# A graph layer whose main path is written out behind no branch, with a ring of 12 slots and x and the results in one buffer

## What is computed

```python
agg = segment_sum(edge_attr, dst, 6250)
h   = relu(concat([x, agg, u[0]], axis=1) @ W1 + b1)      # 128+128+16 -> 256
out = h @ W2 + b2 + x
x   = layernorm(x + out)                                   # over the 128 features, no scale
```

## Time and profile before

| | |
|---|---|
| three runs | 190.38, 191.70, 191.78 us; median 191.7 |
| the profiled execution | span 188.2 us from first to last instruction, 6264 instructions; its time beyond the span is not recorded |
| busy | TensorE 163.8 us (87%), VectorE 117.6 (62%), ScalarE 56.8 (30%), GpSimd 31.7 (17%) |
| DMA | 61.90 MB, mean 329 GB/s; main queue at work for 93.5% of the span |
| chain of waits | TensorE 82%, VectorE 8%, issue 3%, DMA 3%, ScalarE 2% |
| VectorE waits for TensorE's turns | 45.3 us in 44 waits |
| SyncE waits for TensorE's sums | 76.9 us in 43 waits |

### The profile page before, as it was taken

One profiled execution on the slowest core, in us unless ns is written; L12 is line 12 of the kernel. 1 busy time (PEld: TensorE's weight loads), 2 busy tenths in 40 slices (PEclk: granted clock), 3 DMA queues, 4 the chain that ended last, 5 costly groups with the idle time before them and its releaser, 6 DMA issues.

```text
span 188.2 us, 6264 instructions
## 1 busy us (share of the span) xinstructions
PE 163.8 (87%) x2207; PEld 115.0 (61%) x2207; DVE 117.6 (62%) x420; ACT 56.8 (30%) x151; POOL 31.7 (17%) x35
## 2 busy tenths in 40 slices
PE   0057952899999999999999999999999999999890
PEld 0046731548658668568568577487586685777690
DVE  5739693224864775765657666656747757477764
ACT  2022412031441442334144235225314423223331
POOL 7800530000200200201002002002002002006712
PEclk9999998599999999999999999999999999999999
DMA  5999954999999999999999999999999999999402
GB/s 110 307 334 374 376 212 140 384 375 337 337 313 376 373 374 374 370 377 374 374 374 373 374 373 374 374 373 373 374 374 372 374 374 374 356 325 387 164 31 67
DMA packets 42185, 61.90 MB, mean 329 GB/s; under 512 B 1975, under 2 KB 39541, under 8 KB 42170
## 3 DMA queue, kind: packets, MB, share of 16 engines
q1 hardware_dynamic: 41046, 61.23, 93.5%
q10 hardware_dynamic: 1124, 0.48, 1.2%
HBM read 58.50 MB, written 3.20 MB: 328 GB/s over the span
## 4 chain that ended last, share of the span: by engine, by line
PE 82%; DVE 8%; issue 3%; DMA 3%; ACT 2%; DVEq 1%; ACTq 0%
PE sum_ps L966 29%; PE turn_ps L979 15%; PE hid_ps L1024 10%; PE out_ps L1070 9%; PE hid_ps L1031 9%; DMA base_row<-in_dst_dram 3%; PE xt_ps L987 2%; PE hid_ps L1043 2%; PE hid_ps L1007 2%; DVE bases L660 2%; DVE onehot L683 1%; PE xt_ps L1070 1%; DVE place L703 1%; DVE local_rows L668 1%; ACT local_t L475 1%
## 5 line engine op out<-in xcount | busy, mean ns | idle before, releaser
L966 PE MATMUL sum_ps<-edge_ring,onehot 128*32 128x128 f32 x1662 | 62.5, 283 | 6.2 <-issue 4.4
L966 PEld LDWEIGHTS sum_ps<-edge_ring,onehot 128*32 128x32 f32 x1662 | 43.0, 112 | 28.7 <-issue 15.5
L712 DVE TENSOR_TENSOR agg_t<-agg_t,turn_ps 128x128 f32 x70 | 19.9, 284 | 45.3 <-PE turn_ps L979 45.3
L683 DVE TENSOR_TENSOR onehot<-iota,local_t 128x384 f32<-128x384 f32 x70 | 38.3, 551 | 11.7 <-issue 9.2
L496 ACT COPY sums<-sum_ps 128x128 f32<-128x128 f32 x70 | 18.8, 268 | 82.4 <-PE sum_ps L966 80.8
L979 PE MATMUL turn_ps<-place,sums 128*128 128x128 f32 (+1 forms) x140 | 34.6, 329 | 0.0
L433 POOL TENSOR_TENSOR xb<-x_sb,half_b 128x512 f32<-128x512 f32 x10 | 12.8, 1277 | 120.0 <-DVE y L737 120.0
L979 PEld LDWEIGHTS turn_ps<-place,sums 128*128 128x128 f32 (+1 forms) x140 | 21.3, 191 | 13.8 <-issue 13.7
L703 DVE TENSOR_SCALAR place<-iota,rel_cols 128x128 f32<-128x128 f32 x70 | 21.1, 301 | 1.7 <-issue 1.7
L1070 PE MATMUL out_ps<-w_sb,hid_t 128*128 128x128 f32 x160 | 21.0, 275 | 0.0
L1024 PE MATMUL hid_ps<-x_t,w_x 128*128 128x512 f32 x40 | 20.4, 630 | 0.0
(11 more groups left out here) (92 smaller groups left out, 111.6 us busy)
## 6 DMA issues: line engine op xcount, KB each, us to landing
edge_ring<-in_edge_attr_dram SPq DMA_DIRECT2D x69, 768.0 KB, 7.2
x_sb<-in_x_dram SPq DMA_DIRECT2D x10, 256.0 KB, 4.9
out_dram<-z SPq DMA_DIRECT2D x1, 2304.0 KB
dst_rows<-in_dst_dram SPq DMA_DIRECT2D x1, 384.0 KB
x_late<-in_x_dram SPq DMA_DIRECT2D x1, 384.0 KB
out_dram<-z_late SPq DMA_DIRECT2D x3, 128.0 KB
out_dram<-z SPq DMA_DIRECT2D x1, 256.0 KB
w_x<-in_L_gnn_W_dram ACTq DMA_DIRECT2D x1, 128.0 KB, 5.0
```

Of the source, the lines that this page charges most:

```text
L683: nc.vector.tensor_tensor(onehot[:, slot], cols, loc, ALU.is_equal).then_inc(onehot_ready, 1)
L712: nc.vector.tensor_tensor(to, to, turn_ps[i % 2][:, 0:SPAN], ALU.add).then_inc(group_added, 1)
L966: last = nc.tensor.matmul(sum_ps[i % 2][c * WIN:(c + 1) * WIN, 0:d], onehot[0:p, i % ONEHOTS, c * R + r], edge_ring[0:p, i, c * R + r], st ...
```

## The change

- The main path has no branch ahead of it and no loop: all 70 groups are written out, step by step. The flag's branch, with a general path that recomputes everything, stands behind the last work of each engine. The check's steps stand at steps 4 to 6 and 9 instead of 0 to 4.
- The ring has 12 slots. SyncE loads group 0 ahead of the second piece of the destinations.
- `x_all` holds x of all nodes, loaded without a wait. GpSimd adds half of b2 in it, y and the normalised rows are written over it, and the result is stored from it.
- Groups are taken in batches of `PAIR` = 1. One-hots and places have 3 buffers; at step b VectorE makes the one-hot of b+2 and the place of b+1, then adds group b-1.
- A block's x and aggregate parts stand together in the step in which it is complete, the output in the next step, the moments behind the step after, the normalisation one step later. ScalarE's root stands ahead of that step's copy.
- The blocks are complete at groups 6, 12, 18, 24, 30, 36, 40, 46, 52 and 59.
- The late pieces' x is loaded at group 53 and turned at steps 58 to 60; its part is multiplied beside the aggregate part. All normalisations are VectorE's.

```diff
+SLOTS = 12
+PAIR = 1
+BUFFERS = 3
-ONEHOTS = 6
-PLACES = 3
-EARLY = 2
-LEAD = 4
...
+    complete_at = [6, 12, 18, 24, 30, 36, 40, 46, 52, 59, 60, 63, 66, 67, 69, n_grp]
...
+    single0 = 60
+    batch_first = list(range(0, single0, PAIR)) + list(range(single0, n_grp)) + [n_grp]
...
+    hidden_step = [batch_first.index(complete_at[n]) for n in range(n_big)]
+    out_step = [b + 1 for b in hidden_step]
+    turn_x_step = [1] + out_step[:n_big - 1]
...
 # SyncE
+            load_group(0)
+
...
+            for g in range(1, n_grp):
+                load_group(g)
+                if g in x_load_at:
+                    load_x(x_load_at[g])
+                if g == x_late_at:
+                    load_x_late()
...
 # ScalarE
+            for b in range(late_step):
+                for n in range(n_big):
+                    if out_step[n] + 2 == b:
+                        root(n)
+                copy_batch(b)
...
+                for n in range(n_big):
+                    if turn_x_step[n] == b:
+                        copy_x_t(n)
+                    if hidden_step[n] == b:
+                        relu(n)
...
 # VectorE
+            def make_onehot(b):
+                g, k = batch_first[b], len(groups(b))
+                if b >= BUFFERS:
+
+                    dve.wait_ge(group_summed, batch_first[b - BUFFERS + 1])
...
+            def step(b):
+                if b == WORST_STEP + 1:
+                    check(3)
+                if b + 2 < n_batch:
+                    make_onehot(b + 2)
+                if b + 1 < n_batch:
+                    make_place(b + 1)
+                if b > 0:
+                    add_batch(b - 1)
+
+            late_step = batch_first.index(single0)
+            for b in range(late_step):
+                step(b)
+                if CHECK0 <= b < CHECK0 + 3:
+                    check(b - CHECK0)
+                for n in range(n_big):
+                    if out_step[n] + 1 == b:
+                        moments(n)
+                    if out_step[n] + 2 == b:
+                        normalize(n)
...
 # TensorE
+            for b in range(late_step):
+                sum_batch(b)
+                if b > 0:
+                    turn_batch(b - 1)
...
+                if b == WORST_STEP:
+                    pe.wait_ge(worst_ready, 1)
+                    pe.wait_ge(y_ready, 1)
+                    nc.tensor.transpose(out_ps[0:1, worst_at], worst[0:n_grp, 0:1],
+                                        ident[0:n_grp, 0:n_grp]).then_inc(worst_turned, 1)
+                for n in range(n_big):
+                    if out_step[n] == b:
+                        sum_out(n)
+                    if turn_x_step[n] == b:
+                        turn_x(n)
+                    if hidden_step[n] == b:
+                        sum_hidden_x(n)
+                        sum_hidden_a(n)
...
```

More of the change, by code:

```diff
@@ L66, in gnn_resnorm_kernel @@
+    assert n_grp <= P and agg_cols >= n_nodes - 1 + SPAN
+    n_big = 10
+    late0 = n_big * BLOCK
     half = BLOCK // 2
-    rest0 = late0 + 3 * half + 2 * P
+    rest0 = n_nodes // P * P
     rest_nodes = n_nodes - rest0
-    assert 0 < rest_nodes <= P
-    pieces = [(b * BLOCK, P, J) for b in range(full)]
+    rest_cut = rest_nodes // 16 * 16
+    assert rest0 == late0 + 3 * half + 2 * P and 0 < rest_nodes <= P
+    pieces = [(b * BLOCK, P, J) for b in range(n_big)]
     pieces += [(late0 + h * half, P, J // 2) for h in range(3)]
@@ L89, in same @@
[L89 to L104, removed]
+    n_pieces = len(pieces)
+    A, B, C_, D, E, REST = range(n_big, n_pieces)
@@ L344, in _ @@
+            sp.wait_ge(normalized, LAST)
+            store(0, LAST)
+            for n in range(LAST, n_pieces):
+                sp.wait_ge(normalized, n + 1)
+                store(n, n + 1)
             sp.wait_ge(flag_ready, 1)
@@ L519, in relu_late @@
[L519 to L534 removed]
+                last.then_inc(x_t_ready, 1)
@@ L566, in _ @@
             with act.If(general > 0):
-                with act.Fori(1, x_steps + 1) as k:
-                    keep_late_x(k)
-                def mlp(n):
-                    if same(n, REST):
-                        relu_rest()
-                    elif is_late(n):
-                        relu_late(n)
-                    else:
-                        for m in range(m_chunks):
-                            relu(n, m)
-                    if not is_late(n) and not same(n, LAST):
-                        copy_x_t(n + 1)
-                    root(n)
@@ new lines, in turn_batch @@
+            def turn_batch(b):
+                pe.wait_ge(batch_copied, b + 1)
+                pe.wait_ge(place_ready, b + 1)
+                if b >= 2:
+                    pe.wait_ge(group_added, batch_first[b - 1])
+                w = C * WIN if b < n_batch - 1 else WIN
+                for i in range(len(groups(b))):
+                    last = nc.tensor.matmul(turn_ps[b % 2][:, i * SPAN:(i + 1) * SPAN], sums[0:w, b % 2, i],
+                                            place[0:w, b % BUFFERS, i], start=True, stop=True)
+                last.then_inc(batch_turned, 1)
```

1006 lines of the change are left out of this document (430 added, 576 removed).

## The result

The changed kernel takes 197.03 us (median of 195.71, 195.78, 198.28 and 198.56), the kernel before 191.74 beside it: a ratio of 1.0305, with an interval of 1.0224 to 1.0386. Its four times lie on two levels, with spans of 194.0 and 194.1 us and of 196.6 and 196.7; the profile is of one at the upper level.

What follows compares the result with a forecast made beforehand. The prediction took TensorE's queue to bound the kernel and summed −6.0 + 16.4 + 5.5 + 0 = +15.9 us; on a span of 188.2, plus 3.5 from span to median, that gave 207.6 us, range 198 to 214.

Steps and rivals of the forecast that it cites:

- Start, −6.0: Up to group 12: standstill, late transposes and slow clock go, VectorE waits come in; group 12 starts 6.0 us earlier.
- The wait in each block, 1.72 us: Steps 2 to 5 of a block: VectorE's chain takes 6.56 us against TensorE's 4.84, so TensorE waits 1.72 us.
- Base registers, 1.0 us in three places: Later stretches of groups 12 to 60: loading base registers on VectorE, between moments and normalisation, costs 1.0 us.
- End, +5.5: From group 60 on: late pieces' x parts (3.9 us) and output blocks behind the relu; 5.5 us later, between 3 and 8.
- The branch, 0: At the kernel's end: flag and jump lie beside the last store and its landing; 0 us, at most 2.
- Root: ScalarE's root ahead of step 3's copy: about 0.9 of the 1.72 us shows as the turn's wait on that copy.
- From span to median, 3.5: Whole kernel: the median run lies 3.5 us above the profiled span, and the same is added to the forecast.
- Rival (a): Middle blocks: VectorE keeps up and the 1.72 us wait vanishes; 188 to 189 us; chance 0.09 faster, 0.04 same.
- rival (b): Middle blocks: only one place waits or statistics overlap more; 0.8 us per block, 197 to 201 us; chance 0.12.
- (c): Instruction fetches of written-out code stop TensorE, or VectorE falls behind another microsecond per block; 216 to 220 us; chance 0.09.
- (d): The flag is set, so everything is computed a second time, several times slower; chance under 0.01.
- (e): Loop's seven backward branches each hide TensorE's 4.37 us; written out, 31 us go, giving 177 us; chance under 0.01.

Runs made afterwards that it cites:

- b2: The kernel before with its main path only: nobody waits for or loads the flag, code for unsorted destinations left out; 184.21 us, ratio 0.9633.
- e5: The changed kernel with a ring of 6 slots instead of 12; 197.92 us, ratio 1.0315 to the kernel before.
- e8: e6 with a ring of 6 slots instead of 12; 186.76 us, ratio 0.9753 to the kernel before.
- e7: The changed kernel without its branch: flag computed but not loaded, code for unsorted destinations left out; 197.34 us, ratio 1.0272 to the kernel before.
- e1: The changed kernel with ScalarE's root moved behind step 3's copy of the sums; 196.13 and 198.71 us, no ratio.
- e2: The changed kernel with one-hots made 4 groups ahead in 6 buffers; 195.01 us, ratio 1.0188 to the kernel before.
- e3: The changed kernel with a block's normalisation moved to the step in which the next block is complete; 194.17 us, ratio 1.0133 to the kernel before.
- e4: The changed kernel with root behind the copy, one-hots 4 ahead and normalisation at the next block's step; 187.46 us, ratio 0.9796 to the kernel before.
- e9: The changed kernel with root behind the copy and normalisation at the next block's step, one-hots still 2 ahead; 189.17 us, ratio 0.9865 to the kernel before.
- e11: The changed kernel with eight extra unread matmuls on TensorE before its first sums; 195.86 us, ratio 1.026 to the kernel before.
- e6: e4 with the check of the destinations begun at group 6 instead of 4; 186.44 us, ratio 0.9731 to the kernel before.

## Why the prediction was right in sign and wrong in size

Trace against trace the terms are −6.5, +11.3 and +3.5 us, together 8.4 (188.2 to 196.6), against −6.0, +16.4 and +5.5, together 15.9.

The mechanism on which I decided held: both waits stand where they were placed, for the reasons given. What failed is the size of terms. The largest step that failed is the price of loading the base registers, 1.0 us in each of three stretches, where the loads cost 0.12 (3.5 us, with the smaller wait of the same stretches); then come the way from span to median (3.1 us), an end in which work was counted twice (2.0), and a wait per block of 1.72 us that measured 1.23 (1.6 in four blocks). All four make the forecast too long, so nothing evened them out.

- **Start, −6.0: right (−6.5), and for its main reason.** b2 shows the flag's part alone, 5.9 us. Its size is partly luck, since two errors nearly cancel. The first sums are not delayed by 1.5 us (15.03 against 15.14), and the check's reductions cost 2.6 us instead of 3.2. But from the first sums to group 12 it is 27.85 us instead of 26.7: the x transposes and sums up to 23 us run slowly, which I had not counted.
- **Ring and x in one buffer, 0: right** (e5, e8).
- **The wait in each block, 1.72 us: right in place and cause, too large; measured 0.87 + 0.36 = 1.23.** The term of 6.56 us for steps 2 to 5 is 6.22. From the rows above: add 80.97, y 81.18, one-hot 83.10 (1.92 for 2.00), reciprocal 83.93 (0.83 for 0.86), next one-hot 85.17 (1.24 for 1.38), sums 85.78 (0.61 for 0.70). The price of the normalisation held a wait: reciprocal to rows was 0.35 us (80.59 to 80.94, 0.18 of it idle) and is 0.21 now. Why the other three are smaller no row shows. Steps 0 and 1 took 8.08 for 8.15. Four blocks: 1.6 us too much.
- **Base registers, 1.0 us in three places: wrong, and the largest miss.** Those stretches take 6.34, 6.33 and 6.61 us instead of 7.6. VectorE in the first of them:

```profile
124.47 0.28 DVE L603 TENSOR_SCALAR place<-iota,rel_cols 128x128 f32<-128x128 f32 x1
124.78 0.29 DVE L630 TENSOR_TENSOR agg_t<-agg_t,turn_ps 128x128 f32 x1
```

  The loads stand between the two: 0.31 us, where a block without loads has 0.19 (83.54 to 83.73). So they cost VectorE 0.12. The idle time of 0.93 before the one-hot at 78.20 holds something else: it is the first one-hot behind a jump back to the loop's start. VectorE in the kernel before, at the first one-hot behind the loop, with the same six loads ahead of it and no jump back:

```profile
157.90 0.56 DVE L683 TENSOR_TENSOR onehot<-iota,local_t 128x384 f32<-128x384 f32 x1 [0.40 <-issue]
```

  The first pass of the loop, entered without a jump back, shows 0.40 too (at 50.92); the seven after a jump back show 0.91 to 0.97. So more than half of the price was the loop's own, which the changed kernel doesn't have. 3.5 us too much: 22.8 forecast for the three, 19.3 measured.
- **End, +5.5: too large, measured +3.5.** From group 60 to the start of the last output it is 28.03 us now and 25.25 before, +2.8. TensorE's busy time in these stretches grows from 24.45 to 27.01, 2.6 where the forecast had 3.9 for x parts. Each piece was priced well (0.87 for 256 columns against 0.94), but half of the last whole block was counted twice. TensorE in the kernel before:

```profile
158.93 1.02 PE L1024 MATMUL hid_ps<-x_t,w_x 128*128 128x512 f32 x2
159.79 1.02 PE L1031 MATMUL hid_ps<-agg_t,w_a 128*128 128x512 f32 x2
```

  These are half of its x part and half of its aggregate part, 1.81 us together, behind group 60 then and ahead of it now. The forecast put the whole block ahead of group 60 and did not take this half off the end: 3.9 − 1.8 = 2.1 of the 2.6 measured; the rest is small pieces, the last transposes (0.18) among them. The waits grow from 0.80 to 1.02 instead of by 1.75. **The branch, 0: too low by 0.8** (e7).
- **Root: "mending only one of the two would give nothing"**: true of the root (e1), false of VectorE's side (e2 and e3 give 0.34 and 0.43 us of 1.23).
- **From span to median, 3.5: wrong.** The profiled execution of the kernel before was one of its shorter ones: in later runs a span of 188.2 goes with 190.06 us, and one of 189.9 with 191.76. A span lies mostly 1.7 to 1.9 us below its time, in a few executions up to 2.8. The changed kernel's profile fell on its upper level, 1.25 above the median. So the time lies 0.4 us above the profiled span and not 3.5: 3.1 us too much. With the 7.5 of the terms this is the whole distance: 207.6 − 197.0 = 10.6.

Rival (a), that VectorE keeps up, fell; rival (b), a smaller wait at 197 to 201 us, is where the time lies, but not for its reason: both places wait, with 1.23 us rather than the 0.8 it was built on, and the rest is the other terms. Rivals (c) and (d) fell. So did (e): written out, the middle without its waits takes 13.07 us a block (e4), 0.30 less than the loop, and 0.38 was forecast from the late x part alone. The Trainium skill (Runtime: NRT & Kernel Launch, section Instruction fetch mechanics) charges a taken branch with a stall when its target lies outside the fetched window. The traces agree for the one forward jump: 4.37 us in TensorE's way (the flag was written at 28.42 us, before TensorE's last turn ended at 29.34, so this is the flag's load and the jump and no wait for the check), or 0.8 behind the last store. At the loop's jumps back TensorE shows no pause and VectorE 0.5 us more than without one. The prediction read the rule as one for every taken branch and called it refuted by the loop; that does not follow, since the rule asks where the target lies, and no run shows whether the loop's start had left the window.

## What to carry to other kernels

Where two engines take turns, spread the slow one's long instructions over the steps in which the other has most to do. Two of them in neighbouring short steps cost 1.23 us a block here, although VectorE was busy for only 59% of the span; moving the normalisation and the root gave back 0.9 of it (e9). A branch costs where an engine stands before it: leave it at the end. And before an idle time is used as the price of one thing, look for a place where that thing stands alone: here 0.93 us held a jump beside the loads, and the loads cost 0.12.

## What the runs showed of the hardware

- At the start sums take 1.51 us although the granted clock is 1.00 in the same stretch (below, for the changed kernel: stretch, busy time of each engine, clock, share, GB/s); eight matmuls ahead of them bring the first 48 from 2.79 to 2.02 us (e11). So the double duration is not always to be read from the clock's row.

```profile
15.00:19.00 4.00, 3.97 (x53) 3.39 (x53) 2.33 (x8) 0.74 (x3) 0.00 (x0) 1.00 1.06 374
```

- With those matmuls the low clock turned up elsewhere: 0.57 from 13 to 17 us, 0.83 from 150 to 160.
- Over 15 to 165 us one core's transfers move 373 GB/s in the changed kernel, in e4 and in e6. With 6 slots it is 348 in e5 and 368 in e8, where they wait for slots; single slices of 5 us still reach 372 to 377.
- A jump back to a loop's start costs VectorE 0.5 us in the kernel before (0.91 to 0.97 us idle against 0.40 where the loop is entered or left) and TensorE nothing that can be seen.
